# Two GpSimd operations in a selection round instead of four, with other orders around it

## What is computed

```python
def attn(x, w_gate, w_up, w_down):
    s = silu(einsum('bsh,ih->bsi', x, w_gate))
    k = int(0.5 * I)                        # 688
    _, idx = top_k(-abs(s), k)              # the 688 smallest magnitudes of a token
    s = s with those entries set to 0.0
    s = s * einsum('bsh,ih->bsi', x, w_up)
    return einsum('bsi,hi->bsh', s, w_down)

def ffn(x, W_gate, W_up, W_down):
    return silu(x @ W_gate.T) * (x @ W_up.T) @ W_down.T

x = x + _layernorm(attn(_layernorm(x), ...))
x = x + _layernorm(ffn(_layernorm(x), ...))
```

## Time and profile before

| | |
|---|---|
| median of three runs | 824.23 us (823.82 to 825.26) |
| profiled execution | 826.32 us, of it span 824.5 us |
| PE busy | 782.1 us (95%), mean granted clock 0.979 |
| DVE, ACT, POOL busy | 406.8, 317.2, 184.2 us |

### The profile page before, as it was taken

How to read it: one execution, slowest core, us unless ns; L and a number is a source line. 1 busy time by engine, 2 the same in 40 slices (tenths; PEclk the granted TensorE clock), 3 DMA queues, 4 the chain that set the end, 5 groups by cost and what they waited for, 6 DMA issues and landing times.

```text
span 824.5 us, 9847 instructions
## 1 busy us (share of the span) xinstructions
PE 782.1 (95%) x3593; PEld 655.3 (79%) x3593; DVE 406.8 (49%) x821; ACT 317.2 (38%) x479; POOL 184.2 (22%) x454
## 2 busy tenths in 40 slices
PE   8969899999999997897979999999999999999996
PEld 8858788888888886785957788788887888788884
DVE  7567756567656575466558433243221532242123
ACT  5656555545555535435464322121211311121112
POOL 1544423344433333233341000010000100010001
PEclk9999999999999998998998999999999999999998
DMA  8510022221022220220541400111010210012001
GB/s 277 175 48 5 22 73 74 74 73 48 26 73 74 73 86 14 72 87 14 178 169 52 162 14 14 39 55 35 26 39 0 91 39 1 0 52 77 0 1 51
DMA packets 22338, 51.18 MB, mean 62 GB/s; under 512 B 2320, under 2 KB 5904, under 8 KB 22096
## 3 DMA queue, kind: packets, MB, share of 16 engines
q1 hardware_dynamic: 22288, 50.54, 18.2%
HBM read 42.14 MB, written 16.84 MB: 72 GB/s over the span
## 4 chain that ended last, share of the span: by engine, by line
PE 71%; issue 8%; POOL 8%; ACT 6%; DVE 6%; DMA 0%; POOLq 0%; DVEq 0%; ACTq 0%
PE gu_ps L463 28%; PE gu_ps L413 15%; PE y_ps L442 11%; PE tr_ps L484 11%; ACT junk L601 4%; PE y_ps L484 4%; POOL thr L1206 2%; POOL move L1203 1%; PE tr_ps L427 1%; POOL err L1201 1%; POOL unit L1192 1%; POOL xrstd L1175 1%; POOL delta L1205 1%; DVE hT L861 1%; DVE absv L891 1%
## 5 line engine op out<-in xcount | busy, mean ns | idle before, releaser
L601 ACT ACTIVATE junk<-absv,thr 128x1376 bf16<-128x1376 f32 x96 | 138.6, 1444 | 180.8 <-POOL thr L1206 131.9
L992 DVE TENSOR_TENSOR prod<-gu_ps,prod 128x512 f32<-128x512 f32 (+1 forms) x44 | 30.4, 691 | 184.7 <-PE gu_ps L463 184.7
L442 PE MATMUL y_ps<-down_hi,hT 128*128 128x512 f32 (+1 forms) x352 | 116.0, 412 | 0.0
L413 PE MATMUL gu_ps<-gate_hi,xT 128*128 128x460 f32 (+1 forms) x384 | 112.7, 375 | 0.0
L413 PE MATMUL gu_ps<-up_hi,xT 128*128 128x460 f32 (+1 forms) x384 | 111.9, 373 | 0.0
L442 PE MATMUL y_ps<-down_lo,hT 128*128 128x512 f32 (+1 forms) x176 | 73.7, 419 | 21.3 <-DVE hT L861 21.1
L442 PEld LDWEIGHTS y_ps<-down_hi,hT 128*128 128x128 f32 (+1 forms) x352 | 70.2, 199 | 16.4
L413 PEld LDWEIGHTS gu_ps<-gate_hi,xT 128*128 128x128 f32 x384 | 73.5, 191 | 7.9
L413 PEld LDWEIGHTS gu_ps<-up_hi,xT 128*128 128x128 f32 x384 | 72.9, 190 | 7.8
L413 PE MATMUL gu_ps<-gate_lo,xT 128*128 128x460 f32 (+1 forms) x192 | 73.5, 383 | 4.6 <-DVE xT L855 4.6
L413 PE MATMUL gu_ps<-up_lo,xT 128*128 128x460 f32 (+1 forms) x192 | 73.4, 383 | 4.4 <-ACT prod L608 4.4
(11 more groups left out here) (115 smaller groups left out, 1410.9 us busy)
## 6 DMA issues: line engine op xcount, KB each, us to landing
xin<-x_scratch SPq DMA_DIRECT2D x18, 256.0 KB, 3.1
xin<-in_L_attn_x SPq DMA_DIRECT2D x16, 256.0 KB, 4.1
xres<-in_L_attn_x SPq DMA_DIRECT2D x16, 256.0 KB, 4.7
x_scratch<-xres SPq DMA_DIRECT2D x16, 256.0 KB, 2.0
xres<-x_scratch SPq DMA_DIRECT2D x14, 256.0 KB, 2.8
out<-xres SPq DMA_DIRECT2D x14, 256.0 KB, 2.0
raw<-in_L_ffn_W_gate SPq DMA_DIRECT2D x4, 688.0 KB, 5.0
raw<-in_L_ffn_W_up SPq DMA_DIRECT2D x4, 688.0 KB, 4.6
```

The source lines that it names most:

```text
L413: last = nc.tensor.matmul(dst[:, 0:CW[n]], xt, w, start=(c == 0 and i == 0), stop=(c == KC - 1 and i == 2))
L442: last = nc.tensor.matmul(y_ps[:, :], h, w[0:k, c, :], start=(c == 0 and i == 0), stop=(c == JC - 1 and i == 2))
L601: nc.scalar.activation(junk[:, :], absv[:, j % 2, :], ACT.Sign, bias=thr[:, j % 2:j % 2 + 1], scale=-1.0, accum_out=sgn[:, j % 2:j % 2 + 1 ...
L992: nc.vector.tensor_tensor(prod[0:k, 0, GW:2 * GW], bank(("u", idx, 0))[0:k, :], prod[0:k, 0, 0:GW], ALU.mult).then_inc(p2_done, 1)
```

## The change

**A round.** `absv` gets 8 more columns with 3e38 in them, and a count reads 7 of them (`PAD`), so that its sum is the error itself with its sign turned. The first threshold is made on ACT (`guess`), the units, now negative and double buffered, on POOL (`units`). After each of the first five counts ACT waits for its own count and multiplies the sum by the unit (`step`). POOL computes `move` from the count and then adds move times step to the threshold. `thr_done` no longer counts the first threshold. The last gain is 0.4 instead of 0.7.

**Orders.** The rows below show three places. In the first tiles the up products go (0,0), (1,0), (0,1), (0,2), (1,1), (1,2); `transpose_x(2)` stands one product earlier; token tile 3 is normalised long before it is wanted; w_down pieces 13 to 17 are split on DVE behind `select(0)`. For j of 3 to 14 count 4 is written into its own tile's turn; DVE makes, from tile 4 on, `find_below` and `find_top` before the split of the transposed tile, and normalises the next token tile (`x_stats`, `x_normalise`) right behind `select`; POOL has `x_rstd` behind step 0 (tile 3: step 2), `y_rstd` behind step 2, and for `TWO` a second `x_rstd` behind step 3.

```diff
-    GAIN = [1.0, 1.0, 0.7, 0.5, 0.7]
+    GAIN = [1.0, 1.0, 0.7, 0.5, 0.4]
...
+    PAD = int(2 * AIM) - I
+    IA = I + 8
...
-    USEQ = [(0, 0), (1, 0), (0, 1), (1, 1), (0, 2), (1, 2)] + [(j, n) for j in range(2, TILES) for n in range(3)]
+    USEQ = [(0, 0), (1, 0), (0, 1), (0, 2), (1, 1), (1, 2)] + [(j, n) for j in range(2, TILES) for n in range(3)]
...
-            for j, n in USEQ[:5]:
+            for j, n in USEQ[:4]:
                 product(j, 1, n)
             transpose_x(2)
+            product(1, 1, 1)
             product(1, 1, 2)
...
+            def guess(j):
+                act.wait_ge(a_done, j + 1)
+                q = j % 2
+                nc.scalar.activation(thr[:, q:q + 1], asum[:, q:q + 1], ACT.Copy, scale=GUESS / I).then_inc(guess_done, 1)
+
             def count(j, n):
...
+                nc.scalar.activation(junk[:, 0:I + PAD], absv[:, q, 0:I + PAD], ACT.Sign, bias=thr[:, q:q + 1],
+                                     scale=-1.0, accum_out=sgn[:, q:q + 1]).then_inc(counted, 1)
+                if n < STEPS:
+                    act.wait_ge(counted, COUNTS * j + n + 1)
+                    act.wait_ge(unit_done, j + 1)
+                    nc.scalar.activation(step[:, :], sgn[:, q:q + 1], ACT.Copy,
+                                         scale=unit[:, q, n:n + 1]).then_inc(step_done, 1)
...
-            def first_guess(j):
+            def units(j):
...
-                nc.gpsimd.tensor_scalar(unit[:, :], gains[:, :], asum[:, q:q + 1],
-                                        1.0 / (2 * I * I * DENSITY), ALU.mult, ALU.mult)
-                nc.gpsimd.tensor_scalar(thr[:, q:q + 1], asum[:, q:q + 1], GUESS / I, None,
-                                        ALU.mult).then_inc(thr_done, 1)
+                nc.gpsimd.tensor_scalar(unit[:, q, :], gains[:, :], asum[:, q:q + 1],
+                                        -1.0 / (2 * I * I * DENSITY), ALU.mult, ALU.mult).then_inc(unit_done, 1)
...
-                stepped(nc.gpsimd.tensor_scalar(err[:, :], sgn[:, q:q + 1], -1.0, float(2 * AIM - I),
-                                                ALU.mult, ALU.add))
-                stepped(nc.gpsimd.tensor_scalar(move[:, :], err[:, :], err[:, :], float((WINDOW - 1) ** 2) + 0.5,
-                                                ALU.mult, ALU.is_gt))
-                stepped(nc.gpsimd.tensor_tensor(delta[:, :], err[:, :], move[:, :], ALU.mult))
-                nc.gpsimd.tensor_scalar(thr[:, q:q + 1], delta[:, :], unit[:, n:n + 1],
-                                        thr[:, q:q + 1], ALU.mult, ALU.add).then_inc(thr_done, 1)
+                stepped(nc.gpsimd.tensor_scalar(move[:, :], sgn[:, q:q + 1], sgn[:, q:q + 1],
+                                                float((WINDOW - 1) ** 2) + 0.5, ALU.mult, ALU.is_gt))
+                pool.wait_ge(step_done, STEPS * j + n + 1)
+                nc.gpsimd.tensor_scalar(thr[:, q:q + 1], move[:, :], step[:, :], thr[:, q:q + 1],
+                                        ALU.mult, ALU.add).then_inc(thr_done, 1)
```

More of the change, by code:

```diff
@@ L725, in _ @@
                     count(j - 1, 5)
+                guess(j)
                 count(j, 0)
+                if j == 3:
+                    split_x_hi(j + 1)
                 count(j, 1)
-                split_x_hi(j + 1)
                 count(j, 2)
+                if j > 3:
+                    split_x_hi(j + 1)
+                count(j, 3)
                 normalise_y(j - 2)
-                count(j, 3)
+                count(j, 4)
                 if j in TWO:
@@ L734, in _ @@
             last = TILES - 1
-            count(last - 1, 4)
             count(last - 1, 5)
@@ L740, in _ @@
             silu(last, 2)
+            guess(last)
             count(last, 0)
```

164 lines of the change are left out of this document (78 added, 86 removed).

## The result

The changed kernel takes 786.7 us (median of four runs, 785.8 to 787.5) against 824.5 us before (824.2 without the fourth run): a ratio of 0.954, 95% interval 0.952 to 0.956. The forecast was 786.7. Its profiled execution took 787.0 us, with a span of 785.0 us, against 826.32 and 824.5.

The account below looks back on a forecast made before the run. PE was taken as bound, made to wait by a loop of latencies through selection and splits. Gains 12.5 + 0.5 + 19.5 + 5 = 37.5 us off 824.2 gave 786.7; forecast 783 to 793 (0.58), range 779.5 to 801.

Parts of the forecast that it names:

- Parts 1 and 2: Selection: a round of 2.35 to 2.4 us, 0.6 less; first count 0.35 us behind the sum, 1.7 less.
- Part 3: Tiles 4 to 10: with the new orders the loop needs 22.7 us where PE needs 24.3; gain 0.5 us.
- 1.6 us in hand: Tiles 4 to 10: the slack between the loop's 22.7 us and PE's 24.3 us a tile.
- rival B: Slower: `step` and its hops last 1.2 us instead of 0.35, a round 3.2; 836 us; chance 0.05.
- Part 4: Tiles 11 to 14: loop 25.0 us against PE's 24.7, 1.5 us left for new waits; gain 19.5 of 21.0 us.
- Part 5: First tiles: the 4.58 us wait goes, 0.7 of the 4.36 stays, 1.5 of new wait; gain 12.5 us.
- Part 6: Last tiles: a shorter chain to the low part for `down(14)`, 2 us of wait remain; gain 5 us (3 to 8).
- A: Token-heavy tiles keep a third to a half of their waits, the last tiles theirs; 798 to 801 us; chance 0.20.
- C: Selection: the last gain of 0.4 raises a flag and `exact_path` adds some 70 us; 857 us; chance 0.01.
- D: Whole kernel: no new waits at all; 779.6 us; chance 0.10.

Follow-up runs that it names:

- guess_on_pool: The changed kernel with the first threshold made on GpSimd (POOL) again, behind the units as before; 786.2 us, ratio 0.953 to the kernel before.
- one_root: The kernel before with only the second token tile's sums and root moved to the start of the tile in tiles 12 to 14; 809.9 us, ratio 0.983.
- stats_ahead: The changed kernel with the second token tile's sums and root put back at the end of the tile ahead, one step behind the root; 796.9 us.
- orders_only: The changed kernel's orders with the old round, old first threshold and gain 0.7; 800.4 us, ratio 0.970 to the kernel before.
- first_undone: The changed kernel with the rows of tiles 0 to 2 ordered as before on all engines; 792.7 us, ratio 0.961 to the kernel before.
- round_only: The kernel before with the new round and first threshold, all other instructions in their old places; 808.9 us, ratio 0.981.
- late_orders: The changed kernel with only the order around down(14) and down(15) altered, splits of h ahead of late weight splits; 781.1 us, ratio 0.947 to the kernel before.

## Why the prediction was right, point by point

**The time** of 786.7 was met, and part of that is luck. The forecast took 37.5 us off the median. The terms, which were meant for the profiled execution, measured 13.4, 0.4, 20.95, 6.1 and -1.4; in the span 39.5. The profiled execution before was 1.8 us slower than the median before, the one after only 0.3, and so 37.8 is left in the medians. The 2 us of layout, which I hadn't seen, stood against the new wait of `down(15)` with its half clock (2.07 and about 1.6 us), which I hadn't seen either.

**Parts 1 and 2** have the right sizes: a round of 2.42 us where 2.35 to 2.4 was forecast, `step` 0.29 where I took 0.25, the first count 0.27 us behind the sum (0.35). The way to the round was wrong, though. Its threshold that starts 0.75 us sooner would make a round of 2.2; it starts 0.54 sooner (2.05 us behind the count's start, before 2.59). And what sets it is `move` on POOL: `step` on ACT has always ended before it, so its price, which I took for the open one, doesn't enter. The Trainium skill budgets about 0.3 us for an ACTIVATE ahead of its elements (ScalarE: Activation LUTs, "Rules for kernel authors"), which was nearer for `step` than my row of 0.20. The estimate of 2.45 from it was added up wrongly: 0.05 more on 2.37 is 2.42. `guess`, whose scale is a constant, takes 0.20. What I did with the first threshold was wrong: guess_on_pool shows that its 1.7 us a tile buy nothing in sum. It lies in front of the root in the tiles where a root follows, and in front of waits elsewhere.

**Part 3** has the right result (0.4 us, forecast 0.5) from a loop of about the right length (third count 7.5 us behind the sum against 7.7, `below` 15.7 against 16.0). Its "1.6 us in hand" was mis-sized. It counted only the distance from the loop to PE's 24.3 us; measured, a tile hides 4 us, since the wait for the root also takes up delays ahead of it. This made rival B too dear, with harm from 0.3 us a round on: a step 0.5 us longer left these tiles at 24.3, and one 1 us longer gave 812.8, not 835.

**Part 4**, the largest term, was 19.5 against 20.95, and its reason held in both directions (one_root, stats_ahead). Of the 1.5 us left for new waits none came: 24.72 us a tile are PE's own work.

**Part 5** was 12.5 against 13.4. The wait of 4.58 us is gone. The piece of w_down that I expected to hold `silu(2,0)` does, with 0.75 us where I had 0.7; token tile 3's low part costs 0.64 us where I had 1.5.

**Part 6** forecast 2 us of wait at `down(14)`, and it is 2.31. What it left out is the next one: between the low parts of tiles 14 and 15 (393.70 and 413.03) DVE and ACT take 19.3 us, as they did before (432.50 and 451.83, the copies of 14 and 15). POOL has a share in it: its root of tile 14's output and the bias behind it take 1.47 and 0.74 us beside weight splits on DVE (406.15), where they take 0.57 and 0.27 in tile 6 (163.91). Before, PE did not wait for the second, because the longer stall at `down(14)` had put it at half clock behind it (stretch of the kernel before, clock 0.50):

```profile
433.30:437.70 4.40, 4.37 (x10) 3.47 (x11) 4.29 (x12) 2.82 (x4) 0.00 (x0) 0.50 0.36 119
```

At full clock PE is done 2.07 us sooner and waits. The runs bear this out: wherever PE waits for `down(15)` it starts 19.3 us behind `down(14)`, with a wait of 0.44 to 0.49 us where half clock stands behind `down(14)` (orders_only, first_undone, both slower steps) and of 2.07 where it doesn't (changed, round_only, stats_ahead). The stall that was shortened let the next one show; the working asked what comes late for tile 14, and not for tile 15.

**Rivals.** A (the second token tiles keep their waits) didn't occur, nor did C. D, with no wait at all, had 779.6; the variants without the last two waits take 779.5 to 781.1. The order of the last tiles was what stood between, but that the sums agree is partly luck: D had 15 us for the first tiles and 8 for the last ones, and late_orders gains 12.7 and 11.3, some 2 of these by the layout.
